# A new order of a slot's steps in a two-layer pair-product kernel, with loads in three parts

## The reference

```
x: (2048, 39, 16)          W0: (1, 39*39, 128)   W1: (1, 39*128, 128)
x0 = xk = x
for W in (W0, W1):
    Hk = xk.shape[1]
    Wr = W.reshape(39, Hk, 128)
    xk = einsum('bid,bjd,ijh->bhd', x0, xk, Wr)
    outs.append(xk)
result = concatenate(outs, axis=1)       # (2048, 256, 16)
return sum(result, axis=-1)              # (2048, 256)
```

## Time and profile before

| | us |
|---|---|
| median of three runs (lowest to highest) | 660.48 (659.22 to 661.25) |
| the profiled execution's own time | 658.78 |
| its span | 657.0 |
| PE busy in the span | 573.5 |
| DVE, ACT, POOL busy | 477.2, 481.6, 472.6 |
| mean granted TensorE clock | 0.948 of full speed |
| share of the transfer engines, queue 1 | 68.6% |

### The profile page before, as it was taken

One profiled execution on the slowest core, in us unless ns is written; L12 is line 12 of the kernel. 1 busy time (PEld: TensorE's weight loads), 2 busy tenths in 40 slices (PEclk: granted clock), 3 DMA queues, 4 the chain that ended last, 5 costly groups with the idle time before them and its releaser, 6 DMA issues.

```text
span 657.0 us, 13101 instructions
## 1 busy us (share of the span) xinstructions
PE 573.5 (87%) x3176; PEld 498.3 (76%) x3176; DVE 477.2 (73%) x804; ACT 481.6 (73%) x982; POOL 472.6 (72%) x407
## 2 busy tenths in 40 slices
PE   0458778999979998899979997999989999899978
PEld 0247666888868987688968896789968898689968
DVE  4527777788887787688886886878886888878730
ACT  3448787878877887678876887778887788778830
POOL 5668987778866887578875888578876788778700
PEclk9878898899989999799988999899998999999989
DMA  5757888668886687677775776867787677876310
GB/s 217 275 159 233 266 265 260 225 201 269 263 279 190 223 265 269 194 239 254 250 255 196 262 247 204 261 231 219 251 272 250 198 243 257 280 251 216 93 26 17
DMA packets 109081, 148.23 MB, mean 226 GB/s; under 512 B 77648, under 2 KB 86096, under 8 KB 100816
## 3 DMA queue, kind: packets, MB, share of 16 engines
q1 hardware_dynamic: 109008, 147.37, 68.6%
HBM read 134.74 MB, written 2.10 MB: 208 GB/s over the span
## 4 chain that ended last, share of the span: by engine, by line
PE 57%; DVE 14%; issue 11%; ACT 8%; DMA 6%; POOL 1%; ACTq 1%; SPq 0%; DVEq 0%
PE acc L329 9%; PE acc L330 9%; PE acc L331 9%; DMA xr<-xb_dram 5%; PE pg L354 5%; PE fin L366 5%; PE fin L367 5%; PE fin L368 4%; PE pg L355 4%; PE pg L356 4%; DVE fl L555 3%; DVE gl L569 3%; ACT gh L455 3%; PE turn L339 3%; DVE fp L551 2%
## 5 line engine op out<-in xcount | busy, mean ns | idle before, releaser
L644 POOL TENSOR_TENSOR fl<-fs,fh 128x512 fp32r<-128x512 f32 x192 | 256.7, 1337 | 67.0 <-ACT fh L415 66.8
L569 DVE TENSOR_TENSOR gl<-pg,gh 128x320 fp32r<-128x320 f32 x256 | 114.5, 486 | 110.5 <-ACT gh L455 109.6
L329 PE MATMUL acc<-fh,w0h 128*128 128x512 f32 x384 | 163.7, 426 | 25.0 <-DVE w0q L615 16.4
L639 POOL TENSOR_TENSOR fs<-xr,xs 128x512 f32<-128x512 f32 x128 | 163.7, 1301 | 8.7 <-DMA xr<-xb_dram 6.0
L415 ACT ACTIVATE fh<-fp 128x512 fp32r<-128x512 f32 x192 | 115.0, 599 | 63.5 <-DVE fp L551 37.5
L330 PE MATMUL acc<-fh,w0l 128*128 128x512 f32 x384 | 156.7, 408 | 0.0
L331 PE MATMUL acc<-fl,w0h 128*128 128x512 f32 x384 | 156.1, 406 | 0.0
L555 DVE TENSOR_TENSOR fl<-fp,fh 128x512 fp32r<-128x512 f32 x192 | 132.1, 688 | 28.1 <-ACT fh L415 25.8
L415 ACT ACTIVATE fh<-fs 128x512 fp32r<-128x512 f32 x192 | 120.1, 626 | 24.3 <-PE acc L331 19.7
L551 DVE TENSOR_TENSOR fp<-xl,xr 128x512 f32<-128x512 f32 x192 | 127.4, 694 | 13.6 <-DMA xr<-xb_dram 10.0
L354 PE MATMUL pg<-xbd,x1th 128*128 128x320 f32 x256 | 88.0, 344 | 51.4 <-DVE gl L569 32.5
(11 more groups left out here) (35 smaller groups left out, 730.6 us busy)
## 6 DMA issues: line engine op xcount, KB each, us to landing
xr<-xb_dram SPq DMA_DIRECT2D x64, 1536.0 KB, 7.5
xs<-xa_dram SPq DMA_DIRECT2D x64, 256.0 KB, 2.9
xbd<-xdhl SPq DMA_DIRECT2D x512, 20.0 KB, 3.4
xp<-xpairs_dram SPq DMA_DIRECT2D x32, 256.0 KB, 2.7
xdr<-xd_dram SPq DMA_DIRECT2D x64, 80.0 KB, 2.4
outs<-w_dram SPq DMA_DIRECT2D x9, 256.0 KB, 2.9
out_dram<-outs SPq DMA_DIRECT2D x8, 256.0 KB, 2.8
xr<-w0a_dram SPq DMA_DIRECT2D x1, 512.0 KB, 3.3
```

What stands on the lines that cost most here:

```text
L329: nc.tensor.matmul(acc[:, :], w0h[:, t, :], fh[:, t, :], start=t == 0, stop=False)
L569: nc.vector.tensor_tensor(g_at(gl, odd, gi, q), g_psum(odd, q), g_at(gh, odd, gi, q), ALU.subtract).then_inc(g_low, 1)
L639: nc.gpsimd.tensor_tensor(f_at(t), xr[:, gi % 2, t, :], xs[:, gi % 2, :], ALU.mult)\
L644: nc.gpsimd.tensor_tensor(fl[:, t, :], f_at(t), fh[:, t, :], ALU.subtract).then_inc(low_pool, 1)
```

## The change

1. **Slot order.** On PE all four quarters of group g-2 stand in slot g: 0 and 1 at its head, 2 and 3 after tile 1. On ACT `x1_out` is first in a slot, tile 4 comes before tile 3, the quarters' copies stand between the tiles, and `left_out` (the copy `xl` of `xs`) is last. DVE follows suit.
2. **Last contraction.** Five rows in each of slots 1 to 7, four in slot 0 of the chunk after, all behind tile 5.
3. **Loads.** `xr` comes in three transfers of 512 KB, each issued when the two tiles that used its place are multiplied. They are for group g+3 and stand behind `blocks(g)`, with `load_x` and, last, `load_xd(g + 2)`.
4. **Weights.** The first weights come in two parts, so that tiles 0 to 3 can start earlier. The second weights are moved inside DRAM to a scratch tensor (`w1_move`), loaded straight into `w1l` in seven pieces of six rows, and split there; `outs` is free of them.
5. **Loops.** Chunks 0, 1, 6 and 7 are written out; the hardware loop turns twice.

```diff
-            def load_right(j, gi):
-                sp.dma_start(xr[:, gi % 2, :, :], xb[CB * j + gi]).then_inc(xr_in[gi % 2], 16)
+            def load_right(j, gi, u):
+                sp.dma_start(xr[:, gi % 2, 2 * u:2 * u + 2, :], xb[CB * j + gi][:, 2 * u:2 * u + 2, :])\
+                  .then_inc(xr_in[u][gi % 2], 16)
...
+            def w1_move(p):
+                sp.dma_start(w1_copy[:, piece(p), :], w1[:, piece(p), :]).then_inc(w1_moved, 16)
+
             def w1_load(p):
-                n = min(NW, M - NW * p)
+                sp.wait_ge(w1_moved, 16 * (p + 1))
                 if p:
-                    sp.wait_ge(w1_ready, p)
...
+                    sp.wait_ge(w1_in, 16 * p)
+                sp.dma_start(w1l[:, piece(p), :].bitcast(F32), w1_copy[:, piece(p), :]).then_inc(w1_in, 16)
...
-            def chunk(j, first, last):
+            def chunk(j, first, second, last):
                 for gi in range(CB):
                     g = CB * j + gi
-                    if not (last and gi + 2 >= CB):
-                        wait_product(sp, g, 4)
-                        wait_product(sp, g, 5)
-                        load_x(j, gi + 2)
-                        load_right(j, gi + 2)
-                    blocks(g, gi, first)
...
+                    blocks(g, gi, first, last and gi == CB - 1)
+                    if more3:
+                        wait_product(sp, g + 1, 0)
+                        wait_product(sp, g + 1, 1)
+                        load_right(j, gi + 3, 0)
+                    if gi % 2 == 0 and more2:
                         sp.wait_ge(sq_ready, CP * j + gi // 2 + 1)
                         load_pair(CP * j + gi // 2 + 1)
...
+                    if more3:
+                        wait_product(sp, g + 1, 3)
+                        load_right(j, gi + 3, 1)
+                    if first and gi < PIECES:
+                        w1_load(gi)
+                        if gi + 1 < PIECES:
+                            w1_move(gi + 1)
+                    if more3:
+                        wait_product(sp, g + 1, 4)
+                        load_x(j, gi + 3)
+                        wait_product(sp, g + 1, 5)
+                        load_right(j, gi + 3, 2)
+                    if more2:
                         sp.wait_ge(xd_low, g + 2)
                         load_xd(g + 2)
```

More of the change, by code:

```diff
@@ L43, with rows_of, piece @@
 ORDER = (*range(NT), FULL, FULL)
-NW = 4
-PIECES = -(-M // NW)
[L46 to L61, removed]
+HIGH = (0, 1, 2, 4, 3, 5)
+NU = NT // 2
+W0_PART = 4
+W0_FROM = {0: 1, W0_PART: 2, FULL: 3}
+NW = 6
+PIECES = -(-M // NW)
+def rows_of(s):
+    return range(IB * (s - 1), min(IB * s, M))
+def piece(p):
+    return slice(NW * p, min(NW * p + NW, M))
 def pair_slots():
@@ L157, in build @@
         xs_in = [sem("xs_in0"), sem("xs_in1")]
-        xr_in = [sem("xr_in0"), sem("xr_in1")]
+        xr_in = [[sem(f"xr_in{u}{s}") for s in range(2)] for u in range(NU)]
         xp_in = sem("xp_in")
@@ L297, in _ @@
-            load_x(0, 0)
-            load_right(0, 0)
+                    if gi == 2 and not (first or second):
+                        send(j - 2)
+            w0_load(0)
+            load_x(0, 0)
+            load_right(0, 0, 0)
+            w0_load(1)
+            load_right(0, 0, 1)
+            load_right(0, 0, 2)
+            load_pair(0)
             load_xd(0)
-            load_pair(0)
             load_x(0, 1)
+            load_right(0, 1, 0)
             sp.dma_start(idn[:, :], ident).then_inc(ident_in, 16)
-            sp.wait_ge(w0_ready, 2)
@@ L370, in final, with chunk @@
                         last.then_inc(fin_done, 1)
-            def chunk(j, first, last, odd):
+            def chunk(j, first, second, last, odd):
                 for gi in range(CB):
                     g = CB * j + gi
-                    if not first:
-                        final(j - 1, not odd, rows_of(gi, False))
+                    fresh = first and gi == 0
+                    if not (first and gi < 2):
+                        for q in (0, 1):
+                            g_tile(j, gi - 2, q, first and gi == 2)
+                    main(j, gi, 0, fresh)
+                    main(j, gi, 1, fresh)
                     if not (first and gi < 2):
@@ L460, in final_out, with w1_high_part, chunk @@
                 nc.scalar.activation(outs[:, 1, :], fin[:, 0:NB], COPY).then_inc(out2_ready, 1)
[L462 to L472, removed]
+            def w1_high_part(p):
+                act.wait_ge(w1_in, 16 * (p + 1))
+                nc.scalar.activation(w1h[:, piece(p), :], w1l[:, piece(p), :].bitcast(F32), COPY).then_inc(w1_high, 1)
+            def chunk(j, first, second, last, odd):
                 for gi in range(CB):
@@ L478, in chunk @@
                     was_odd = odd if gi > 1 else not odd
+                    if prev:
+                        x1_out(g - 1, first and gi == 1)
                     if prev2:
@@ L481, in chunk @@
                         g_high_part(j, gi - 2, 1, was_odd, None)
-                    if prev:
-                        x1_out(g - 1, first and gi == 1)
+                    if more:
+                        high(g + 1, 0, False)
                     if gi % 2 == 0:
@@ L495, in chunk @@
                     if more:
-                        high(g + 1, 3, False)
                         xd_split(j, gi + 1, first and gi == 0)
                         high(g + 1, 4, False)
+                        high(g + 1, 3, False)
+                    if gi == 1 and not (first or second):
+                        final_out(j - 2)
+                    if first and 0 < gi <= PIECES:
+                        w1_high_part(gi - 1)
+                    if more:
+                        high(g + 1, 5, False)
```

248 lines of the change are left out of this document (133 added, 115 removed).

## The result

The changed kernel takes 785.47 us (783.42 to 792.49), the one before 659.85 (656.98 to 661.25) beside it: ratio 1.193 (1.184 to 1.202), a fifth slower. The forecast, 692 us, has the sign; the time is 50 us above its range. The profiled execution has a span of 784.2 us.

What follows compares the result with a forecast made beforehand. PE bound the kernel before (busy 87%, floor 8.35 us a slot); after, a loop through the late `xdr` would. 104 to group 7, 558 middle, 28.4 tail and 1.8 outside the span gave 692 us, range 645 to 735.

Steps and rivals of the forecast that it cites:

- loop over two slots: Steady slots: copy of `acc`, blocks, loads, landing of `xdr`, ACT back to copy of `acc`; 20.0 us, 10.0 a slot.
- head: Start to the copy of `acc` of group 0: 23 us, against 34.3 before, a gain of 11.
- steps 2 and 4: Loop legs: SP issuing the eight blocks, 5.4 us; ACT from the split of `xdr` to the copy of `acc`, 2.7.
- Chunk 0: First chunk's seven slots at 11.7 us: copy of `acc` of group 7 at 104 us, bounds 92 to 112.
- The middle: From the copy of `acc` of group 7 to group 63, 56 slots: 558 us against 522.4 before.
- Step 1: Loop leg from the copy of `acc` to the first block's issue, after quarter 3 on PE: 3.2 us, 1.6 before.
- longer: Rival, chance 0.07: PE's waits halve its clock, adding 28 us; with the `xdr` landing leg at its upper end, 745 us.
- Step 3: Loop leg from first `xr` part's issue to `xdr` landing: 8.7 us with `xp`, 8.1 without; bounds 7.3 to 11.6.
- `xdr` in time: Rival, chance 0.10: no wait for `xdr`, PE's order rules at 8.5 us a slot, 598 us in all.
- SP is the bound: Rival, chance 0.05: SP's issues of blocks and loads set the slot at 8.8 us, 618 us in all.
- Fixed time for each part: Rival, chance 0.01: each `xr` part pays its own fixed transfer time, 54 x 2 us more, 800 us.
- All eight slots alike: Sign of being right: all slots of a chunk alike, near 10 us, in pairs of 20.

Runs made afterwards that it cites:

- Run 1: Changed kernel with the load of `xdr` issued directly behind the eight blocks, ahead of the parts of `xr`: 645.57 us, ratio 0.972 to the kernel before.
- run 2: Changed kernel with ACT's copy of `fin` to `outs` in slot 1 moved ahead of the copy of `xdr`: 769.05 us, ratio 1.165 to the kernel before.
- run 3: Changed kernel with `xr` in one transfer of 1536 KB again, issued behind `xs` at the last part's place: 794.88 us, ratio 1.207 to the kernel before.
- run 4: Changed kernel with 32 unused 256-column filler matmuls on PE at the head of every even slot: 779.21 us, ratio 1.180 to the kernel before.
- run 8: Changed kernel with the `fin` copy ahead of the `xdr` copy and 32 filler matmuls in even slots: 730.25 us, ratio 1.106 to the kernel before.
- run 9: Changed kernel with the load of `xp` cut to 32 of its 512 columns, squares left out: 763.13 us, one run, only its trace used.
- Run 10: Changed kernel with the load of `xp` moved behind that of `xdr`, nothing else: 723.06 us, ratio 1.093 to the kernel before.
- run 6: Changed kernel with `xdr` and `xs` directly behind the blocks, `fin` copy ahead, `xr` in one transfer and `xp` last: 618.45 us, ratio 0.934 to the kernel before.
- run 5: Changed kernel with `xdr`, then `xs`, directly behind the blocks, then three `xr` parts, and `fin` copy ahead: 634.69 us, ratio 0.962 to the kernel before.

## Why the prediction was right in sign and wrong in size

**The mechanism** was right: the late `xdr` closes a loop over two slots. Run 1 opens it with two lines and gains 140 us; runs 2 to 4 and 8 to 10 leave `xdr` behind and keep the wait. The head (23.7 for 23), the tail (27.8 for 28.4), steps 2 and 4 came out as worked. Chunk 0 ended 5 us late (109.2 for 104), inside its bounds.

**The middle** was forecast at 558 us and took 647, 89 more. The pairs took 22.5 us for 20.0, which is 70 us in 28 pairs, and slot 1 adds the rest:
- *Step 1, 3.2 us, was mis-sized: 4.4.* That is 34 us. It was summed from pitches at full clock. The forecast spread PE's wait evenly, 1.6 us in each slot; in fact the loop leaves one slot of a pair full and puts the whole wait, 3 us and more, at one place, behind which the clock is down. In the turn above step 1 took 3.4 us at clock 1.00 and 5.4 at 0.50. Run 8 holds the clock up: step 1 is 3.5 there, and the kernel is 39 us faster than run 2, step 3 being 0.4 us a pair shorter too. The rival "longer" named this mechanism, with a chance of 0.07 and a price of 28 us; that was the wrong case to make unlikely.
- *Step 3, 8.7 us, was mis-sized: 9.9.* 1.2 us in each of 28 pairs is 34 us. It was taken from the median landing of one `xr` of 1536 KB, plus 0.8 for `xp` and `xdr` at 424 GB/s. In slots without `xp` it took 7.65 (8.1 forecast), in slots with it 9.9: 2.3 us more, and not 0.6. Run 10 puts `xp` last and gets 1.6 of that back; run 9 leaves its place and takes its bytes, for 0.8. The other 0.7 stay in these slots with `xp` behind `xdr`, so its place does not make them. Why the place costs more than the bytes is open: the second part of `xr` lands 2.8 us behind its forerunner in the slots with `xp` and 1.4 in the others, with a small `xp` as well (2.6), and no run isolates why.
- *A wait that the prediction did not have*: the first row of the last contraction for ACT's copy of `fin`, behind the wait for `xdr`. The prediction listed three tiles, `xl` and the copy of `acc` as queued behind that wait and left the copy of `fin` out. Run 2: 16 to 19 us.

34 + 34 + 19 = 87, against 89; steps 2 and 4 cancel. The terms are not independent, as run 8 shows, so this is an account and no exact split.

**A premise.** "All transfers go through one queue in order" holds in the traces for the landings of the large loads among each other. Blocks do not keep to it: some landed up to 3.1 us before an `xr` or `xdr` issued ahead of them, in the kernel before and in the changed one. The loop rests on `xdr` behind `xr`, where the order held.

**The rivals.** "`xdr` in time", 598 us, is what run 6 comes near to with `xdr` moved, at 618: its slot is 8.70, not 8.5. "SP is the bound" was real, but hidden: run 5 has it, with 9.06 us a slot against the 8.8 put down. "Fixed time for each part" fell with run 3; its 800 us lay near the result for a reason that is not its own. The prediction's top of the range, 735, came from bounds of step 3 alone: "a mean over many slots should stay under 10.8" a slot held for step 3 (9.9 is within its 7.3 to 11.6) and failed since step 1 was given no bounds at all. The 745 us of the rival "longer" is too low by its own terms: 692, 28 for the clock and 54 times 0.8 for slots of 10.8 make 763.

**The signs** named ahead: ACT's copy of `xdr` is the row held longest by a transfer, and SP waits at `g_done`, both as forecast. "All eight slots alike" was wrong, and is the sign of what was missed.

## What to carry to other kernels

The large loads on one queue landed here in the order of issue, so a small load that something needs in the next slot belongs ahead of the large ones that are needed two slots later; write the queue's order by due time, and count each issue of the engine that issues. Where a closed loop sets the pace, list everything that is queued on each engine behind its wait, and give bounds to each leg, those on compute engines too. A loop over two slots need not share its wait between them: sum it once with all the wait in one slot, and with the clock that PE has after such a pause. Filler work on an engine is free only at the places where that engine waits; look for the wait at each of them, not at one.

## What the runs showed of the hardware

- PE's granted clock went from 1.00 to 0.50 over one pause: PE had been busy throughout 329.00 to 333.40 and was then idle 3.2 us; the 512-column matmuls from 337.23 on had pitches of 0.43 instead of 0.23 us, and two tiles and two quarters took 2 us more. Useless matmuls in the pause (run 8) made the kernel 39 us faster than without them (run 2).
- Three queued transfers of 512 KB take as long as one of 1536 KB (15.5 and 15.6 us with the blocks ahead, run 3), but each costs SP 0.5 to 0.6 us to issue (324.25 to 327.10 in the kernel after); with 8 blocks and up to 6 loads in a slot SP itself was the bound at 9.06 us a slot (run 5).
- An 80 KB load directly behind the small blocks lands after 2.4 us in the median (run 1), and after 6.2 in the median, up to 8.3, behind the parts of `xr` (kernel after).
- 20 KB blocks, which write 16 partitions each, can land up to 3.1 us before a larger load issued ahead of them on the same queue; the larger loads kept their order (kernels before and after).
